# Mask seeds on ScalarE, a split first masked batch, and feed-forward batch 0 begun inside layer one

## The chip, the cores and the metric

The kernel runs on one core of one Trainium2 chip. Its time is the device time of one execution in microseconds (us). Before the change the median of three runs is 509.7 us (509.5 to 510.54). TensorE is called PE here, VectorE DVE, ScalarE ACT, GpSimd POOL, and SP is the queue that issues most of the DMAs.

## The reference

Eight batches of 256 tokens with 128 features go through four residual blocks:

```python
x = x + xattn0(layernorm(x), ctx)          # layer one: 16 heads of 8, no mask
x = x + ffn0(layernorm(x))                 # quantised linear, 3-tap conv, SiLU, quantised linear
x = x + xattn1(layernorm(x), ctx, mask)    # layer two: logits + mask * -1e9
x = x + moe(layernorm(x))                  # 8 experts, top 2 of them per token
```

`ffn0` rounds the layer-normed activations to integers per token (`act_quant`), multiplies by ternary weights into 512 hidden channels, convolves each channel over three neighbouring tokens, applies SiLU, rounds again and multiplies back to 128. In `xattn1` every logit gets `mask * -1e9` before its softmax.

## The kernel before

Every engine runs one hand-written program in order; semaphores are the only ties between engines. What stands later in an engine's program cannot start before what stands ahead of it, so the order of the lines is the schedule.

**Attention.** `attention_tensor`, `attention_scalar`, `attention_vector`, `attention_gpsimd` and `attention_sync` each run bodies b = -1, 0, ... 7 and a tail (b = 8, 9). A body has 16 steps n, one for a head. The table `STEPS` says at which step each other stage of a body is issued, one number for each layer. In step n PE computes `scores(b+1, n)` (L1658, two matmuls of 128x256 into banks 0 and 1 of PSUM), from which DVE takes the row maxima (L1289; L1303 with a mask in layer two). Once per half batch POOL splits these maxima (L817, L819), PE transposes them (L1635), ACT copies them (L967) and a DMA writes them into the stack of queries. Then `shifted(b, n)` recomputes the scores transposed, with the maxima subtracted (L1743, banks 2 to 4), ACT takes the exponential (L1023), and PE multiplies four heads at once with the values (`weighted_v`, L1698). In layer two `shifted` first puts the mask there: one matmul of 128x512 (L1740) with `start=True`, and the two of L1743 add to it. Between these stand, once per batch, the projections of queries and keys (L1618, L1619; high parts on ACT, L1052, or L954 outside the loop; low parts on DVE, L1313) and of values (L1781), the normalised output's transposes (L1852, L1860) and projection (L1867), which makes the new residual (L1282). Its layer norm is made by DVE (statistics, L428 to L434), POOL (`ln_power`, L439, L441) and DVE again (`ln_apply`, L447); in layer one quantising follows on DVE (L458 to L462) and POOL (L468 to L474).

**Feed-forward.** `ffn_tensor`, `ffn_scalar`, `ffn_vector` and `ffn_rows`/`quant_clip` on POOL run one step for a batch: hidden products (L1671 and, with the taps folded into the weights, L1674 to L1676), the conv's middle tap on ACT (L915, L916), its sides on DVE (L924, L930), SiLU on ACT (L940, L944), transposes (L1954), their largest value on DVE (`quant_scale`, L1510), rounding on ACT (L1155), clipping on POOL (L762), transposes back (L1965), copy (L1162), output (L1974), residual on DVE (L1526) and layer norm. PE runs `int_transposes(b-1)`, `ffn_hidden(b+2)`, `output(b-1)`, `tokens(b-2)`, `act_transposes(b+1)` in a step. The last steps are written out; the query and key products of layer two's first batch stand in them (`qk_products(eng, 1, 0, ...)`), and so do its first scores, in front of the values.

**After that** layer two runs the attention loop, with the routing of the experts inside, and a loop over 39 tiles of the experts ends the kernel.

The ties that matter around the change, in `shifted`, `extras` and `ffn_silu`:

```python
if n >= back or after(b, 0):
    eng.wait_ge(a.p_sb, b * 16 + n - back + 1)      # PE: bank free once its last exponential is done
if l == 1:
    eng.matmul(ps[:, bank, :], neg_mask_eye[:, :], mask_k[b % 3]..., start=True, stop=False)
if l == 0 and isinstance(b, int) and b == NB and n == 2:
    eng.wait_ge(a.p_sb, NB * 16)                     # PE: hidden(0) only after layer one's last exponential
    for half in range(2):
        ffn_hidden(eng, 0, 0, half)
```

## Time and profile before

| what | value |
|---|---|
| median of three runs | 509.7 us (509.5 to 510.54) |
| the profiled execution: device time / span from first to last instruction | 508.18 us / 506.4 us |
| granted TensorE clock, mean over the span | 0.981 |
| busy over the span: PE / PEld / DVE / ACT / POOL | 443.3 / 363.2 / 345.9 / 301.6 / 226.5 us |
| layer one's steady bodies | about 32 to 152 us |
| its last body, tail and the start of the feed-forward | 152 to 189.4 us |
| the rest of the feed-forward and the start of layer two | 189.4 to 247 us |
| layer two | 247 to 406 us, a body every 20.9 us |
| experts' tiles | 406 us to the end |

Starts in the trace's timeline are microseconds from the first instruction. A matmul's duration there includes the time that its result takes to pass through; the distance from one start to the next tells what it holds PE for. "[0.58 <-POOL max_split L819]" behind a row says that its engine stood idle for 0.58 us ahead of it and which event ended that.

### The profile page before, as it was taken

How to read it: one execution, taken by the hardware profiler on the slowest of the kernel's cores; microseconds unless marked ns; L12 is line 12 of the kernel's file. 1: busy time of each engine (PE TensorE's matmuls, PEld its weight loads, DVE VectorE, ACT ScalarE, POOL GpSimd, SP SyncE). 2: the span in 40 equal slices, each digit the busy share in tenths (PEclk: the TensorE clock that was granted, in tenths of full speed). 3: DMA queues.
4: the chain of work that ended last, by engine and by line, in shares of the span. 5: the costliest groups of instructions: out<-in, count | busy, mean ns of one | idle time of the engine just before them, and what ended most of it. 6: DMA issues, size and time to landing. Idle time of an engine off the chain costs nothing.

```text
span 506.4 us, 11481 instructions
## 1 busy us (share of the span) xinstructions
PE 443.3 (88%) x3709; PEld 363.2 (72%) x3709; DVE 345.9 (68%) x1233; ACT 301.6 (60%) x649; POOL 226.5 (45%) x455
## 2 busy tenths in 40 slices
PE   3689999999998779967999999999999889899960
PEld 2477777777775668856778878777777579899960
DVE  6767787878783267877887788787878266444424
ACT  5237776767767448874466756566556555455630
POOL 4752464123216245767200225354453566666650
PEclk9999999999999989989999999999999999999995
DMA  6463323332405995034253234333320301332107
GB/s 216 150 223 105 115 85 116 102 101 77 137 4 207 426 415 213 2 105 130 84 159 113 88 107 158 118 122 94 112 61 2 87 23 39 85 85 82 53 15 249
DMA packets 40698, 61.55 MB, mean 122 GB/s; under 512 B 6121, under 2 KB 30506, under 8 KB 39232
## 3 DMA queue, kind: packets, MB, share of 16 engines
q1 hardware_dynamic: 38080, 56.20, 34.0%
q0 software_dynamic: 2272, 4.24, 2.6%
q8 instruction: 30, 0.49, 0.4%
q10 hardware_dynamic: 288, 0.39, 0.3%
q14 instruction: 28, 0.23, 0.2%
HBM read 31.45 MB, written 29.23 MB: 120 GB/s over the span
## 4 chain that ended last, share of the span: by engine, by line
PE 45%; DVE 10%; issue 5%; ACT 4%; DMA 3%; SPq 2%; POOL 1%; POOLq 0%; DVEq 0%; ACTq 0%
PE ps L1698 6%; PE ps L1658 6%; PE ps L1740 6%; PE ps L1743 5%; PE ps L1889 5%; PE ps L1900 5%; ACT probs L1023 2%; PE ps L1867 1%; DMA k_blocks<-y_dram 1%; DVE ps L1303 1%; PE ps L1954 1%; PE ps L1674 1%; SPq L544 1%; PE ps L1675 1%; PE ps L1676 1%
## 5 line engine op out<-in xcount | busy, mean ns | idle before, releaser
L1023 ACT ACTIVATE probs<-ps 128x512 f32<-128x512 f32 x256 | 147.0, 598 | 79.6 <-PE ps L1743 75.0
L1658 PE MATMUL ps<-k_blocks,q_stacks 128*128 128x256 f32 x512 | 117.9, 314 | 6.4 <-DVE row_max L1289 3.0
L1289 DVE TENSOR_REDUCE row_max<-ps 128x2 f32<-128x512 f32 x144 | 94.9, 686 | 26.9 <-PE ps L1658 25.7
L1743 PE MATMUL ps<-q_stacks,k_blocks 128*128 128x256 f32 x512 | 104.9, 288 | 1.2 <-DMA q_stacks<-maxT 1.0
L1303 DVE CUSTOM_DVE_ANT_0 ps<-ps,mask_q 128x256 f32<-128x256 f32 x224 | 89.8, 452 | 20.6 <-PE ps L1658 18.9
L1743 PEld LDWEIGHTS ps<-q_stacks,k_blocks 128*128 128x128 f32 x512 | 86.8, 189 | 20.8 <-issue 10.6
L1658 PEld LDWEIGHTS ps<-k_blocks,q_stacks 128*128 128x128 f32 x512 | 82.6, 197 | 13.9 <-issue 4.3
L1698 PE MATMUL ps<-probs,v_aug 128*32 128x256 f32 x1024 | 68.5, 385 | 4.3 <-ACT probs L1023 3.1
L817 POOL TENSOR_SCALAR max_split<-row_max 128x16 fp32r<-128x16 f32 x32 | 6.5, 204 | 124.3 <-issue 93.0
L1740 PE MATMUL ps<-mask_k,neg_mask_eye 128*128 128x512 f32 x128 | 54.5, 426 | 0.0
L739 POOL DMA_INDIRECT y_dram<-x_ring x39 | 39.1, 1003 | 22.6 <-ACT x_ring L1102 14.2
L1698 PEld LDWEIGHTS ps<-probs,v_aug 128*32 128x32 f32 x1024 | 27.8, 109 | 24.1 <-ACT probs L1023 6.2
L1889 PE MATMUL ps<-m_xT,m_w 128*128 128x128 f32 x312 | 41.8, 277 | 2.9 <-DVE m_w L1449 1.7
L1900 PE MATMUL ps<-conv_out,m_h 128*128 128x128 f32 x312 | 41.2, 276 | 0.0
L1889 PEld LDWEIGHTS ps<-m_xT,m_w 128*128 128x128 f32 x312 | 37.9, 192 | 4.1 <-DVE m_w L1449 3.0
L1455 DVE COPY conv_out<-experts 128x512 f32 x39 | 18.3, 469 | 31.2 <-PE ps L1900 31.1
L729 POOL DMA_INDIRECT slots_dram<-rows,r_slot x32 | 32.4, 1011 | 13.8 <-issue 7.8
L1900 PEld LDWEIGHTS ps<-conv_out,m_h 128*128 128x128 f32 x312 | 37.9, 192 | 0.0
L1740 PEld LDWEIGHTS ps<-mask_k,neg_mask_eye 128*128 128x128 f32 x128 | 24.0, 188 | 12.8 <-issue 11.9
L1303 DVE DVE_READ_ACCUMULATOR2_ANT row_max<- 128x1 f32 x224 | 31.9, 142 | 0.0
L439 POOL TENSOR_SCALAR ln_ve<-ln_mv 128x2 f32<-128x2 f32 x24 | 5.8, 240 | 52.4 <-DVE ln_mv L434 52.3
L1090 ACT ACTIVATE m_xT<-ps 128x128 f32<-128x128 f32 x39 | 10.8, 277 | 25.1 <-PE ps L1880 25.1
(217 smaller groups left out, 760.1 us busy)
## 6 DMA issues: line engine op xcount, KB each, us to landing
slots_dram<-x_ring SPq DMA_DIRECT2D x1, 10400.0 KB, 30.1
q_stacks<-q_dram SPq DMA_DIRECT2D x32, 256.0 KB
k_blocks<-k_dram SPq DMA_DIRECT2D x128, 48.0 KB
q_dram<-qk_parts SPq DMA_DIRECT2D x16, 256.0 KB, 2.9
k_dram<-qk_parts SPq DMA_DIRECT2D x16, 256.0 KB, 2.9
mask_in<-host_mask SPq DMA_DIRECT2D x8, 512.0 KB, 3.6
experts<-host_experts SPq DMA_DIRECT2D x1, 4096.0 KB, 39.1
x_ring<-slots_dram SPq DMA_DIRECT2D x39, 65.0 KB
```

The source lines that it names most:

```text
L729: eng.indirect_dma_start(out=slots_dram[:, :], out_offset=bass.IndirectOffsetOnAxis(ap=r_slot[r][:, k, i:i + 1], axis=0), in_=rows[:, r, k ...
L739: eng.indirect_dma_start(out=y_dram[:, :], out_offset=bass.IndirectOffsetOnAxis(ap=x_ring[:, slot, D:D + 1].bitcast(U32), axis=0), in_=x_r ...
L1023: eng.activation(probs[:, n // HPS % 2, n % HPS, :, :].rearrange("p k q -> p (k q)"), ps[:, head_bank(BANKS_T, n)[0], :], ACT.Exp).then_in ...
L1289: eng.tensor_reduce(row_max[:, :, n], ps[:, head_bank(BANKS_S, n)[0], :].rearrange("p (i k) -> p i k", i=NT), AX.X, ALU.max).then_inc(a.s_ ...
L1303: last = eng.tensor_tensor_reduce(out=scored, in0=scored, in1=mask_q[t % 2][:, i, :], scale=1.0, scalar=-3.0e38, op0=ALU.add, op1=ALU.max, ...
L1455: eng.tensor_copy(m_down[:, j % 2, :, :].rearrange("p c d -> p (c d)"), experts[:, bass.ds(weight_at[j] + EH, EC * D)]).then_inc(m_weights, 1)
L1658: mm = eng.matmul(ps[:, bank, i * S:(i + 1) * S], q_stack[r][:, st, i * P:(i + 1) * P], k_blocks[r][:, st, j, :], start=not masked, stop=n ...
L1698: mm = eng.matmul(ps[j * HR:(j + 1) * HR, bank, 0:S], v_aug[r][:, k, first:first + HR], probs[:, st % 2, j, k, :], start=(odd == 0 and k = ...
L1740: eng.matmul(ps[:, bank, :], neg_mask_eye[:, :], mask_k[b % 3][:, :, :].rearrange("p i k -> p (i k)"), start=True, stop=False)
L1743: mm = eng.matmul(ps[:, bank, k * S:(k + 1) * S], k_blocks[r][:, st, j, k * P:(k + 1) * P], q_stack[r][:, st, :], start=(l == 0), stop=(l ...
L1889: mm = eng.matmul(ps[:, BANK_W[j % 2], c * P:(c + 1) * P], m_w[:, j % WR, c * P:(c + 1) * P], m_xT[:, j % 2, :], start=True, stop=True)
L1900: mm = eng.matmul(ps[:, BANK_Y[j % 2], 0:D], m_h[:, j % 2, c, :], m_down[:, j % 2, c, :], start=(c == 0), stop=(c == EC - 1))
```

## The change

Seven edits, in the order in which they run:

1. In layer one the transposes of the second half's maxima move from step 0 to step 1, behind `shifted(b, 1)` and ahead of the last `weighted_v` of the batch before; ACT's copy of that `weighted_v`'s result moves from step 0 to step 1.
2. In layer one `ln_apply` moves from DVE to POOL.
3. `ternary_taps` (three POOL operations) moves from body 6 to body 3.
4. The feed-forward's hidden products of batch 0 move into the last body of layer one (chunks 2 and 3 at step 3, chunk 0 at step 6, chunk 1 at step 8); the conv's middle tap of batch 0 goes to DVE, the load of the SiLU table stands right behind the last exponential, and hidden products of batch 1, transposes and `quant_scale` of batch 0 go into the tail.
5. The keys of layer two's batch 0 are projected in feed-forward step 3 and its queries in step 4 (`first_product` into the free half of bank 7, `first_high`, `first_low`, `first_side`), and the product of both in step 5 is gone.
6. The scores of batch 0's heads 0 to 7 are spread over the last three feed-forward steps, their maxima on DVE with them.
7. In layer two, for heads 5, 7, 8, 11, 13 and 15 of each batch the mask matmul on PE is replaced by an ACTIVATE that writes `-MASK_A * mask_k` into the bank (`mask_seed`), on which the two matmuls add; they wait for it.

```diff
-    "max1": (0, 2),
+    "max1": (None, 2),
-    "a_out1": (0, 0),
+    "a_out1": (1, 0),
-    "d_ln": (11, 12),
+    "d_ln": (None, 12),
+        SEEDED = (5, 7, 8, 11, 13, 15)
+        SEED_STEPS = (2, 4, 5, 8, 10, 12)
+        FIRST_SIDES = {3: 1, 4: 0}
...
         attention_gpsimd, body:
                     ln_power(eng, s, b - 1)
+                    if l == 0:
+                        ln_apply(eng, s, b - 1)
-            attention_gpsimd(eng, 0, "main 0", {-1: add_output_bias, 0: routing_constants, 1: ternary, NB - 2: ternary_taps})
+            attention_gpsimd(eng, 0, "main 0", {-1: add_output_bias, 0: routing_constants, 1: ternary, 3: ternary_taps})
...
         attention_scalar, behind the exponential of step n:
+                    if l == 1 and exists(b) and n in SEED_STEPS:
+                        mask_seed(b, SEEDED[SEED_STEPS.index(n)])
+            def mask_seed(b, n):
+                if n == SEEDED[0]:
+                    eng.wait_ge(a.k_k, b + 1)
+                eng.wait_ge(a.p_sb, b * 16 + n - 2 if n < H - 1 else b * 16 + 12)
+                eng.activation(ps[:, head_bank(BANKS_T, n)[0], :],
+                               mask_k[b % 3][:, :, :].bitcast(F32).rearrange("p i k -> p (i k)"),
+                               ACT.Copy, scale=-MASK_A).then_inc(a.t_seed, 1)
...
         attention_tensor, shifted:
-                if l == 1:
+                seeded = l == 1 and n in SEEDED
+                if seeded:
+                    eng.wait_ge(a.t_seed, b * len(SEEDED) + SEEDED.index(n) + 1)
+                elif l == 1:
                     eng.matmul(ps[:, bank, :], neg_mask_eye[:, :], mask_k[b % 3][:, :, :].rearrange("p i k -> p (i k)"),
                                start=True, stop=False)
         attention_tensor, body and extras:
+                    ahead = l == 0 and n == at["pv"] % HPS and exists(b)
+                    if ahead:
+                        shifted(b, r, n)
+                        second_max(b)
+                if l == 0 and b == NB - 1 and n == 3:
                     eng.wait_ge(a.s_max, NB * 16)
+                    eng.wait_ge(f_tern, 9)
+                    ffn_hidden(eng, 0, 0, 1)
+                if l == 0 and b == NB - 1 and n in (6, 8):
+                    ffn_hidden(eng, 0, 0, 0, (n // 2 - 3,))
+                if l == 0 and b == NB and n == 2:
                     eng.wait_ge(a.p_sb, NB * 16)
-                    eng.wait_ge(f_tern, 9)
-                    for half in range(2):
-                        ffn_hidden(eng, 0, 0, half)
-                if l == 0 and isinstance(b, int) and b == NB and n == 8:
-                    ffn_hidden(eng, 1, 1, 0)
+                    ffn_hidden(eng, 1, 1, 1)
+                if l == 0 and b == NB and n == 4:
+                    ffn_hidden(eng, 1, 1, 0, (0,))
...
         ffn_tensor, step:
+                if b in FIRST_SIDES:
+                    eng.wait_ge(fx_new, b - 1)
+                    first_product(eng, FIRST_SIDES[b])
                 if exists(b + 2):
                     ffn_hidden(eng, b + 2, r, 0)
                     ffn_hidden(eng, b + 2, r, 1)
+                if b in FIRST_SIDES:
+                    eng.wait_ge(att[1].qk_lo, 2 - FIRST_SIDES[b])
                 if exists(b - 1):
                     output(b - 1)
...
-            qk_products(eng, 1, 0, BANKS_HEAD[0])
```

**PE, layer one, steps 0 and 1 of a middle body.** `k_blocks,q_stacks` are scores and `q_stacks,k_blocks` shifted scores, `ident_r,max_split` is the transposes of the second half's maxima, and `probs,v_aug` the last `weighted_v` of the batch before. Before:

```order
L1658 MATMUL ps<-k_blocks1,q_stacks 128x256 x2
L1743 MATMUL ps<-q_stacks,k_blocks0 128x256 x2
L1635 MATMUL ps<-ident_r,max_split 8x128 x4
L1658 MATMUL ps<-k_blocks1,q_stacks 128x256 x2
L1698 MATMUL ps<-probs,v_aug1 32x256 x8
L1743 MATMUL ps<-q_stacks,k_blocks0 128x256 x2
```

After:

```order
L1743 MATMUL ps<-k_blocks1,q_stacks 128x256 x2
L1841 MATMUL ps<-q_stacks,k_blocks0 128x256 x2
L1743 MATMUL ps<-k_blocks1,q_stacks 128x256 x2
L1841 MATMUL ps<-q_stacks,k_blocks0 128x256 x2
L1720 MATMUL ps<-ident_r,max_split 8x128 x4
L1783 MATMUL ps<-probs,v_aug1 32x256 x8
L1743 MATMUL ps<-k_blocks1,q_stacks 128x256 x2
L1841 MATMUL ps<-q_stacks,k_blocks0 128x256 x2
```

The transposes and `weighted_v` moved behind the scores and the shifted scores of head 1.

**PE, from the last `weighted_v` of layer one to its projection.** `ffn_w` and `w1_taps` are the feed-forward's hidden products (two matmuls of `ffn_w` or three of `w1_taps` for a chunk or half of one), `ident,o_raw` and `ident,o_norm` transposes of the attention's output, `ident,probs` the transposes of the feed-forward's activations, `w_all,o_normT` the projection. Before:

```order
L1676 MATMUL ps<-xnT_all,w1_taps 128x255
L1671 MATMUL ps<-xnT_all,ffn_w 128x256 x2
L1852 MATMUL ps<-ident,o_raw 128x128 x4
L1860 MATMUL ps<-ident,o_norm 128x128 x2
L1674 MATMUL ps<-xnT_all,w1_taps 128x256
L1675 MATMUL ps<-xnT_all,w1_taps 128x255
L1676 MATMUL ps<-xnT_all,w1_taps 128x255
L1674 MATMUL ps<-xnT_all,w1_taps 128x256
L1675 MATMUL ps<-xnT_all,w1_taps 128x255
L1676 MATMUL ps<-xnT_all,w1_taps 128x255
L1867 MATMUL ps<-w_all,o_normT 128x128 x2
```

After:

```order
L1783 MATMUL ps<-probs,v_aug1 32x256 x8
L1756 MATMUL ps<-xnT_all,ffn_w 128x256 x2
L1955 MATMUL ps<-ident,o_raw 128x128 x4
L1759 MATMUL ps<-xnT_all,w1_taps 128x256
L1760 MATMUL ps<-xnT_all,w1_taps 128x255
L1761 MATMUL ps<-xnT_all,w1_taps 128x255
L1963 MATMUL ps<-ident,o_norm 128x128 x2
L2056 MATMUL ps<-ident,probs 128x128 x8
L1759 MATMUL ps<-xnT_all,w1_taps 128x256
L1760 MATMUL ps<-xnT_all,w1_taps 128x255
L1761 MATMUL ps<-xnT_all,w1_taps 128x255
L1970 MATMUL ps<-w_all,o_normT 128x128 x2
```

Batch 0's hidden products, whose last two rows stand first in the fence of before, are gone from here; batch 1's are spread between the transposes, and batch 0's activations are transposed ahead of the projection.

**ACT, layer two, behind the exponential of head 1 of a middle body.** `probs<-ps` is an exponential, `ps<-mask_k` a seed, `maxT<-ps` the copy of the second half's maxima, `qk_parts` the high parts of a later batch, `v_aug` its values. Before:

```order
L967 ACTIVATE maxT<-ps 8x512
L1023 ACTIVATE probs<-ps 128x512 x2
L1052 ACTIVATE qk_parts<-ps,b_all 128x512 x2
L1023 ACTIVATE probs<-ps 128x512 x4
L1036 ACTIVATE o_normT<-ps 128x256
L1043 ACTIVATE v_aug0<-ps 128x2x16x8
L1023 ACTIVATE probs<-ps 128x512 x2
```

After:

```order
L1016 ACTIVATE maxT<-ps 8x512
L1072 ACTIVATE probs<-ps 128x512
L1131 ACTIVATE ps<-mask_k1 128x512
L1072 ACTIVATE probs<-ps 128x512
L1103 ACTIVATE qk_parts<-ps,b_all 128x512 x2
L1072 ACTIVATE probs<-ps 128x512
L1131 ACTIVATE ps<-mask_k1 128x512
L1072 ACTIVATE probs<-ps 128x512
L1131 ACTIVATE ps<-mask_k1 128x512
L1072 ACTIVATE probs<-ps 128x512 x2
L1087 ACTIVATE o_normT<-ps 128x256
L1094 ACTIVATE v_aug1<-ps 128x2x16x8
```

Three seeds came in, behind the exponentials of heads 2, 4 and 5; three more stand in the second half of the body, behind those of heads 8, 10 and 12.

## Rows read from the trace of the kernel before

**Rows 1.** Busy by stretch (stretch, length, five engines, PEclk, DMA share, GB/s)

```profile
32.00:152.00 120.00, 112.70 (x1063) 87.86 (x1063) 95.66 (x220) 84.81 (x169) 38.94 (x82) 1.00 0.32 97
...
189.40:247.00 57.60, 47.96 (x337) 40.65 (x335) 43.67 (x132) 38.20 (x82) 36.49 (x59) 0.96 0.30 101
...
285.40:306.30 20.90, 20.79 (x184) 16.36 (x178) 17.12 (x88) 12.97 (x28) 4.90 (x19) 1.00 0.37 113
...
388.00:406.00 18.00, 14.44 (x131) 10.32 (x123) 6.61 (x41) 9.92 (x23) 10.43 (x31) 1.00 0.24 61
```

**Rows 2.** Waits of PE, 32 to 152 us (in total, times, longest)

```profile
PE ps L1635 <- POOL max_split L819: 3.1, 6, 0.6
```

**Rows 3.** Timeline, layer one, steps 0 to 1 (start, us, engine, line)

```profile
101.67 0.40 PE L1743 MATMUL ps<-q_stacks,k_blocks 128*128 128x256 f32 x2
...
102.65 0.41 PE L1635 MATMUL ps<-ident_r,max_split 128*8 128x128 f32 x4 [0.58 <-POOL max_split L819]
...
103.38 0.69 DVE L1289 TENSOR_REDUCE row_max<-ps 128x2 f32<-128x512 f32 x1 [0.81 <-PE ps L1658]
```

**Rows 4.** Groups by line and shape (count, busy, mean ns, idle before)

```profile
L1023 ACT ACTIVATE probs<-ps 128x512 f32<-128x512 f32 x256 | 147.0, 598 | 79.6 <-PE ps L1743 75.0
...
L1740 PE MATMUL ps<-mask_k,neg_mask_eye 128*128 128x512 f32 x128 | 54.5, 426 | 0.0
...
L447 POOL TENSOR_SCALAR xn<-x_res,ln_mv,ln_rstd 128x128 f32<-128x128 f32 x16 | 12.7, 798 | 0.9
...
L1155 ACT ACTIVATE probs<-ps,fa 128x512 f32<-128x512 f32 x16 | 10.2, 703 | 3.0 <-DVE fa L1520 3.0
...
L447 DVE TENSOR_SCALAR xn<-x_res,ln_mv,ln_rstd 128x128 f32<-128x128 f32 x16 | 4.8, 344 | 3.1 <-POOL ln_rstd L441 2.5
```

**Rows 5.** Timeline, POOL and DVE side by side, end of the feed-forward

```profile
238.24 1.58 POOL L447 TENSOR_SCALAR xn<-x_res,ln_mv,ln_rstd 128x128 f32<-128x128 f32 x2
...
238.32 1.29 DVE L1289 TENSOR_REDUCE row_max<-ps 128x2 f32<-128x512 f32 x2 [0.23 <-PE ps L1658]
```

**Rows 6.** Waits of PE, 152 to 190 us

```profile
PE ps L1698 <- ACT probs L1023: 2.7, 3, 1.2
```

**Rows 7.** Timeline, tail of layer one and start of the feed-forward

```profile
168.40 1.07 PE L1698 MATMUL ps<-probs,v_aug 128*32 128x256 f32 x16 [1.20 <-ACT probs L1023]
...
172.95 0.60 PE L1852 MATMUL ps<-ident,o_raw 128*128 128x128 f32 x4
...
177.27 0.61 PE L1867 MATMUL ps<-w_all,o_normT 128*128 128x128 f32 x4
...
180.63 0.60 DVE L447 TENSOR_SCALAR xn<-x_res,ln_mv,ln_rstd 128x128 f32<-128x128 f32 x2 [1.27 <-POOL ln_rstd L441]
```

**Rows 8.** Timeline, feed-forward step 5

```profile
216.86 0.59 PE L1618 MATMUL ps<-xnT_all,w_all 128*128 128x256 f32 x2
...
217.73 0.61 PE L1974 MATMUL ps<-w,f_intT 128*128 128x128 bf16 x8
217.93 1.27 ACT L954 ACTIVATE qk_parts<-ps,b_all 128x512 fp32r<-128x512 f32 x2 [0.51 <-PE ps L1619]
```

**Rows 9.** Timeline, a body of layer two

```profile
303.12 0.40 PE L1740 MATMUL ps<-mask_k,neg_mask_eye 128*128 128x512 f32 x1
...
303.36 0.40 PE L1743 MATMUL ps<-q_stacks,k_blocks 128*128 128x256 f32 x2
...
314.71 0.14 DVE L1303 DVE_READ_ACCUMULATOR2_ANT row_max<- 128x1 f32 x1
...
314.90 0.50 PE L1658 MATMUL ps<-k_blocks,q_stacks 128*128 128x256 f32 x2
```

**Rows 10.** Timeline, the last body of layer two

```profile
396.80 0.71 PE L1867 MATMUL ps<-w_all,o_normT 128*128 128x128 f32 x4 [0.33 <-ACT o_normT L1036]
...
399.98 1.58 ACT L1023 ACTIVATE probs<-ps 128x512 f32<-128x512 f32 x3
...
405.01 0.60 DVE L1359 TENSOR_SCALAR rows<-x_res,ln_mv,ln_rstd 128x128 f32<-128x128 f32 x2 [6.00 <-POOL ln_rstd L441]
```

More of the change, by code:

```diff
@@ L496, in stack_landed, with first_side @@
             eng.wait_ge(stack_loaded[half][part], (a.first + b + 1) * STACK_COUNT[part] * DMA)
+        def first_side(eng, a, w):
+            dst = (q_dram[0][:, DH:HR, :], k_dram[0])[w].rearrange("h (d w) q -> h d w q", w=3)
+            eng.wait_ge(a.qk_hi, 2 - w)
+            eng.dma_start(dst[:, :, w:w + 2, :], qk_parts[:, 4 * w:4 * w + 2, :].bitcast(F32)).then_inc(a.to_dram, DMA)
+            eng.wait_ge(a.qk_lo, 2 - w)
+            low = 2 - 2 * w
+            eng.dma_start(dst[:, :, low:low + 1, :], qk_parts[:, 2 + w:3 + w, :].bitcast(F32)).then_inc(a.to_dram, DMA)
+            hold(eng, a.to_dram, (2 - w) * 2 * DMA)
+            for half in range(2):
+                sets = slice(2 * half, 2 * half + 2)
+                if w == 0:
+                    q_load(eng, 0, half, sets)
+                else:
+                    k_loads(eng, 0, half, sets)
         def parts_store(eng, a, t):
@@ L1615, in pre_transposes, with first_product @@
             mm.then_inc(ln_pre.xT, 1)
+        def first_product(eng, w):
+            if w == 1:
+                eng.wait_ge(att[0].mT_sb, NB * 2)
+                eng.wait_ge(wq_scaled, 2)
+            else:
+                eng.wait_ge(ln_f0.xs, 1)
+                eng.wait_ge(att[1].qk_lo, 1)
+            eng.matmul(ps[:, BANK_M, S:2 * S], (wq, wk)[w][1][:, :], one((xnT_all, ctxT)[w], 0),
+                       start=True, stop=True).then_inc(att[1].qk_ps, 1)
         def qk_products(eng, l, t, bank):
@@ L1667, in ffn_hidden @@
             x = one(xnT_all, b)
-            for c in range(2 * half, 2 * half + 2):
+            for c in chunks or range(2 * half, 2 * half + 2):
                 h = hidden_ps(r, c)
```

177 lines of the change are left out of this document (105 added, 72 removed).

## The prediction

> **What bounds the kernel now.** I read the busy time by stretch first [rows 1]. In a steady body of layer two PE is busy for 20.79 of 20.90 us at full clock (1.00), DVE for 17.12, ACT for 12.97: PE sets the length and ACT has 7.9 us to spare. In layer one's steady bodies PE is busy for 112.70 of 120 us, so a few waits remain. In the feed-forward (189.4 to 247 us) no engine passes 48 of 57.6 us: chains through all engines decide there. In the last body of layer two (388 to 406 us) there are no scores any more, PE is busy for 14.44 of 18 us and waits for ACT and for POOL.
>
> Then the waits. Layer one's largest wait of PE is the one for POOL's split of the maxima, 3.1 us in six waits [rows 2]; the timeline of one body shows it as the 0.58 us ahead of the transposes, while DVE stands idle 0.81 us until the scores behind them [rows 3]. The groups by line give prices [rows 4], the timelines show the places. Idle time of ACT in layer two is no reserve lying in one piece: 75.0 of its 79.6 us ahead of exponentials are waits for PE's shifted scores [rows 4], a slice of each head.
>
> **Layer one's transposes (edit 1).** PE now has the scores and shifted scores of head 1 ahead of the transposes. From 101.67 the old row order gave 0.40 us of work and then 0.58 us of wait; the new order puts two pairs there, some 0.7 us, and the split is done by then. The scores come 1 us earlier than before, so DVE's 0.81 us gap closes too. What comes late next is the copy of the maxima on ACT, wanted only by the second half of the body. I take 0.5 us for each of six bodies (of 0.58): **-3.0 us**. Bounds: 0, if the maxima that the next body waits for end no earlier, and 6 x 0.81 = -4.9, if DVE was the chain.
>
> **ln_apply on POOL (edit 2).** Per batch two operations of 344 ns leave DVE and two of 798 ns come to POOL [rows 4]: the result is 0.9 us later. In the steady bodies nobody waits: DVE reached its own later than POOL had finished the power, since the operation stood at a step of the body. In the tail DVE waits for POOL already (its start at 180.63 us) [rows 7], so there +0.95. POOL's queue behind it holds the split of the maxima, several us later.
> The Trainium skill ("SBUF — State Buffer", "SBUF: two separate sides") says that DVE and GpSimd share a port pair that one of them holds for a whole instruction, which speaks against more POOL work; it limits this to DVE operations of certain kinds. Where POOL's 1.58 us of ln_apply and two row maxima ran side by side, these took 1.29 us together [rows 5], no more than one alone twice (0.69 us) [rows 3]. So the trace shows no such stop for the maxima, DVE's main work in layer one. By the rule read without its limit the six bodies and the last one would lose up to 7 x 1.6 = 11 us; that is a rival below, with a small chance.
>
> **Ternary taps (edit 3).** Some 5 us of POOL move to a body where POOL is mostly idle (38.94 of 120 us) [rows 1]: 0.
>
> **Start of the feed-forward (edit 4).** Between the last weighted_v (168.40) and the projection (177.27) lie 8.9 us [rows 7]: 1.0 of weighted_v, 3.55 of hidden(0) up to the transposes at 172.95 (eight pieces of 0.44: three for each of two chunks, one for each of the other two), then these, a wait for the normalising, its transposes, and six pieces of hidden(1). In the new order this stretch holds 1.0 + 0.9 (two pieces) + 0.45 (four transposes) + 1.3 (three pieces, filling the wait) + 0.3 + 1.0 (the activations' eight transposes) + 1.3 (three pieces) = 6.2 us: -2.7. Hidden(0) is 3.5 us in the body before, which has 2.7 us of waits for exponentials [rows 6]; its chunks at steps 3, 6 and 8 meet only part of them, and ACT, which sets that body's pace there, gets its shifted scores a little later. So at least 0.8 comes back, and I take 1.4. With the +0.95 of ln_apply the chain to the first layer-normed batch gains 0.35; the activations' transposes ahead of it gain more. I take **-0.6 us** at the start of the steps, between -2.5 (transposes decide) and +1.5 (the chain through POOL decides, and a PE that waits more runs at a lower clock: 0.96 in the stretch behind) [rows 1].
>
> **First batch split (edits 5 and 6).** Step 5 loses the products (216.86 to 217.73, 0.87 us on PE) and the high parts on ACT (1.27 us) [rows 8] that stood ahead of the rounding chain, and the low parts on DVE: I take -1.4 of these. Steps 3 and 4 each gain one product of 0.43 us, one ACTIVATE of half the size on ACT and one operation on DVE, and output waits for the latter: +0.5 each. SP's loads for the first half of the heads leave earlier and nobody waits for them. The scores spread over the last steps fill PE's waits, but three more row maxima of 0.69 us stand ahead of the last residual on DVE; the last output waits for its copy anyhow. I take -0.5 for that. Together -1.4 + 1.0 - 0.5 = **-0.9 us**, between -2 and +1.5 (the new wait for the low parts holds PE's queue, with output, tokens and transposes behind it, in both steps). The chain from the last residual through POOL to the first shifted scores is unchanged and moves as a whole.
>
> **Seeds (edit 7).** A mask matmul holds PE from 303.12 to 303.36 [rows 9], 0.24 us; six a body are 1.44, and 48 in all are 11.5. What they cost ACT no row shows: no ACTIVATE here writes PSUM. From below it is the distance of exponentials back to back, 1.58 us for three [rows 10], 0.49 each; from above the rounding's 703 ns of the same size [rows 4]. I take 0.55, near the exponentials, the same 128x512 in the other direction. That is 3.3 us a body, 12.97 + 3.3 = 16.3 of some 19.9 us: ACT stays under PE. Each seed stands three steps ahead of its head but cannot run before that bank's exponential; PE reaches the head two heads later, over 2 us, so its wait on the seed is normally over. Behind a seed on ACT wait the next exponential and, behind that, weighted_v.
> Yet not all is gained. The scores of head 7 start at 314.90, right behind DVE's row maximum of 314.71 [rows 9]: in that part DVE decides, and what head 5 saves is lost. Of heads 7 and 8 I count 0.35, of heads 11, 13 and 15 0.6, as exponentials pushed back by a seed delay weighted_v there. 0.95 for each of seven bodies is -6.65. In the last body PE waits for exponentials and gains nothing from less work; seeds of heads 13 and 15 (2 x 0.5, and 0.25 for their own waits) stand ahead of the rank copy, from which POOL's chain runs to the rows at 405.01, for which DVE stood idle 6.00 us [rows 10]: +1.25. Sum **-5.4 us**, between -11.5 and +4 (each seed holding PE for 0.08 us more than it saves).
> The Trainium skill ("ScalarE: Activation LUTs", "Step-by-step: what each stage is for") says that ScalarE reaches PSUM faster than SBUF. No row of this case shows it; by it the seeds would sit at the lower bound of 0.49 us or under it, ACT would have 0.4 us a body more to spare, and the sum would move towards the first rival's.
>
> **Sum.** -3.0 - 0.6 - 0.9 - 5.4 = -9.9 us. The profiled execution took 508.18 us (506.4 span and 1.8 around it); it becomes 498.3. The median of the runs stands 1.5 above it, so 509.7 - 9.9 = **499.8 us**. The experts' tiles, with no edit, only move.
>
> **Rivals.**
> 1. The seeds are paid in full: PE is busy without a gap in layer two [rows 1], so each removed matmul shortens the body. Seven bodies save 7 x 1.44 = 10.1, the last one loses 0.5: -9.6 in place of -5.4, 495.6 us. Against it: row maxima that PE already waits for [rows 9].
> 2. ACT and DVE take the seeds' gain back, layer two 0: total -4.5, 505.2 us. For it: DVE is at 17.12 of 20.9 and not evenly spread; against it: 7.9 us of idle ACT.
> 3. The edges lose: body 7 and the POOL chain give +1.5, steps 3 and 4 +1.5, in place of -1.5 together; 504.3 us.
> 4. Slower than before: the seeds make ACT's order the bound. Shifted scores wait in PE's queue for the seed, behind them the scores for DVE, and the exponential that frees the bank stands behind the seed again. It decides from the point where each seed holds PE for 0.24 + 4.5/48 = 0.33 us; at a whole seed, 0.55, it is 48 x 0.31 = +15, less 4.5: 520 us; at 0.45 it is 515.
> 5. POOL's ln_apply stops DVE, as weighed above: 11 - 9.9 = +1, 511 us.
>
> **Chances.** My forecast (497 to 503) 0.52, rival 1 0.15, rival 2 0.14, rival 3 0.09, rival 4 0.07, rival 5 0.03. About 1 us (0.2%) is what can be told from no change here. Slower: rivals 4 and 5 but for some of 5, 0.08; within 0.2%: the rest of 5 and the poor end of rivals 2 and 3, 0.04; faster 0.88. The range runs from below rival 1 to above rival 2, 494 to 506.5: outside lie rivals 4 and 5 and the full sum of all lower bounds.
>
> **What would show it.** Right: layer two's bodies at about 19.9 us with PE still busy nearly throughout, ACT at 16 us, seeds of about 0.55 us; no wait for the split in layer one and bodies 0.5 us shorter; the last body of layer two longer by a microsecond, with POOL's slots later. Wrong: shifted scores that wait for ACT's seeds, scores that wait for row maxima more than before, bodies still at 20.9 us, a DVE that stands while POOL applies the norm, or steps 3 and 4 longer by more than 1 us.

## The result and the profile after

The changed kernel takes 506.12 us (median of 5 runs, 504.78 to 507.69), the kernel before 510.54 us (5 runs, 509.5 to 511.55): ratio 0.9924, 95% interval 0.9899 to 0.9949. By the ratio that is some 3.9 us less, by the two medians 4.4. Forecast were 9.9 us less and 499.8 us. The profiled execution of the changed kernel took 505.85 us with a span of 504.0 us, 2.4 us less than the span of before.

The busy time by stretch, with the columns of [rows 1], in stretches that answer to those:

```profile
32.00:152.00 120.00, 115.06 (x1076) 89.55 (x1075) 94.69 (x211) 87.06 (x173) 53.92 (x100) 1.00 0.32 97
...
190.00:245.00 55.00, 46.10 (x329) 39.08 (x329) 41.95 (x128) 34.56 (x73) 35.61 (x58) 0.96 0.28 92
...
282.60:302.90 20.30, 19.87 (x180) 15.25 (x174) 17.01 (x88) 15.98 (x34) 4.90 (x19) 1.00 0.37 111
...
384.00:403.00 19.00, 12.96 (x117) 8.90 (x120) 5.83 (x38) 13.70 (x30) 10.00 (x27) 0.98 0.24 62
```

A steady body of layer two takes 20.4 us now, not 20.9 and not the 19.9 that I had forecast. ACT is at 15.98 us in it (16.3 forecast), and PE, which was busy for all but 0.1 us, stands idle for 0.43. In the stretch of the last body, taken 1 us longer here, PE is busy for 1.5 us less and ACT for 3.8 us more.

I took the starts of a few marks from the timelines of two executions of each kernel (the second of each is an experiment below) and set the distances from one mark to the next side by side. "Projection" is the matmuls of L1867, which stand at L1970 after the change; "activations" the transposes of L1954, L2056 after. All in us:

| from, to | before, 1st | before, 2nd | changed, 1st | changed, 2nd |
|---|---|---|---|---|
| start to layer one's first projection | 59.08 | 61.24 | 59.13 | 58.17 |
| five bodies of layer one | 86.50 | 86.47 | 84.15 | 84.12 |
| two more projections (last body, tail) | 31.69 | 31.70 | 31.04 | 31.03 |
| last projection to activations of batch 2 | 16.65 | 15.60 | 18.22 | 18.46 |
| to the last residual of the feed-forward | 41.38 | 40.99 | 39.79 | 39.78 |
| to layer two's first projection | 39.70 | 39.70 | 40.18 | 40.18 |
| five bodies of layer two (the fifth is shorter) | 103.40 | 103.29 | 100.68 | 100.72 |
| to the next-to-last projection | 18.40 | 18.37 | 18.38 | 18.37 |
| to the last projection | 15.13 | 17.28 | 18.53 | 18.50 |
| to the end | 94.47 | 94.46 | 93.90 | 94.37 |
| span | 506.4 | 509.1 | 504.0 | 503.7 |

Most rows repeat within about 0.1 us. Three do not for one and the same kernel: the start (up to 2.2 us), the stretch behind layer one's last projection (1.05 us), and the one to the last projection (2.15 us); two more, the one to the last residual and the one to the end, differ by 0.4 to 0.5 us in one of the kernels.

The lines behind the rows that changed, in the order of the program. Steps 0 and 1 in a body of layer one, as in [rows 3] (timeline: start, duration, engine, line):

```profile
100.87 0.48 PE L1743 MATMUL ps<-k_blocks,q_stacks 128*128 128x256 f32 x2
...
101.20 0.23 POOL L855 TENSOR_TENSOR max_split<-row_max,max_split 128x16 fp32r<-128x16 f32 x1
...
101.57 0.39 PE L1720 MATMUL ps<-ident_r,max_split 128*8 128x128 f32 x4
```

POOL's split ends at 101.43, while PE still works on head 1, and the transposes follow without a wait. The waits of [rows 2] are gone; the largest that is left of PE's waits between 32 and 152 us is for row maxima (total, times, longest), and it was there before the change with 2.1 us:

```profile
PE ps L1743 <- DVE row_max L1349: 1.9, 6, 0.4
```

The start of the feed-forward, against [rows 7]:

```profile
168.23 1.07 PE L1783 MATMUL ps<-probs,v_aug 128*32 128x256 f32 x16 [1.19 <-ACT probs L1072]
...
174.32 0.61 PE L1970 MATMUL ps<-w_all,o_normT 128*128 128x128 f32 x4
...
177.75 1.59 POOL L452 TENSOR_SCALAR xn<-x_res,ln_mv,ln_rstd 128x128 f32<-128x128 f32 x2
...
181.94 1.43 POOL L479 TENSOR_SCALAR xn<-xn,qa 128x128 f32<-128x128 f32 x2 [0.21 <-POOL xn L476]
183.46 0.62 POOL L810 TENSOR_SCALAR mask_k<-mask_in 128x512 fp32r<-128x512 int32 x1
...
183.52 0.44 PE L485 MATMUL ps<-ident,xn 128*128 128x128 f32 x2 [3.26 <-POOL xn L479]
...
184.86 1.31 POOL L796 TENSOR_SCALAR f_int<-probs 128x512 bf16<-128x512 int16 x2
...
185.53 0.61 PE L2068 MATMUL ps<-ident_bf,f_int 128*128 128x128 bf16 x4 [1.57 <-POOL f_int L796]
```

The projection follows the last weighted_v by 6.1 us instead of 8.9. But behind it PE runs out of work: it stands 3.26 us until POOL has applied the norm and quantised batch 7, and 1.57 us more until POOL, after two mask operations, has clipped batch 0's integers. The transposes of these integers follow the projection by 11.22 us; before the change it was 11.32 us in the first trace and 10.59 in the second, with PE at work for most of that time. From there to the activations of batch 2 PE has the same rows of work, but at a lower granted clock (PEclk, the column behind POOL). Before and after:

```profile
188.59:193.92 5.33, 5.33 (x33) 4.70 (x32) 2.72 (x8) 5.01 (x12) 1.23 (x2) 0.82 1.05 450
```

```profile
185.53:192.54 7.01, 6.92 (x32) 5.59 (x33) 1.36 (x4) 3.59 (x8) 1.84 (x3) 0.64 0.99 427
```

In the second traces it is 5.01 us at 1.00 before and 7.27 us at 0.61 after.

The costs of edits 2 and 7, by line and shape (count, busy, mean ns, idle before), against [rows 4]:

```profile
L1838 PE MATMUL ps<-mask_k,neg_mask_eye 128*128 128x512 f32 x80 | 33.7, 422 | 0.0
...
L1131 ACT ACTIVATE ps<-mask_k 128x512 f32<-128x512 f32 x48 | 28.7, 598 | 1.8
...
L452 POOL TENSOR_SCALAR xn<-x_res,ln_mv,ln_rstd 128x128 f32<-128x128 f32 x32 | 25.6, 805 | 1.8
```

A seed takes 598 ns (0.55 forecast) and ln_apply on POOL 805 ns.

A body of layer two, behind the seeded head 11:

```profile
316.70 0.40 PE L1841 MATMUL ps<-q_stacks,k_blocks 128*128 128x256 f32 x2
...
316.93 0.40 PE L1720 MATMUL ps<-ident_r,max_split 128*8 128x128 f32 x4
...
317.32 0.14 DVE L1363 DVE_READ_ACCUMULATOR2_ANT row_max<- 128x1 f32 x1
...
317.51 0.51 PE L1743 MATMUL ps<-k_blocks,q_stacks 128*128 128x256 f32 x2 [0.18 <-DVE row_max L1363]
```

The shifted scores of head 11 start 0.24 us earlier than before within the body, for want of the mask matmul. The next scores then wait 0.18 us, until DVE's row maximum of 317.32 has ended (317.46): the gain is given back on the spot. In [rows 9] DVE was late only at head 7.

The last body, against [rows 10]:

```profile
390.39 0.47 PE L1841 MATMUL ps<-q_stacks,k_blocks 128*128 128x256 f32 x2 [0.48 <-ACT ps L1131]
...
391.57 0.71 PE L1970 MATMUL ps<-w_all,o_normT 128*128 128x128 f32 x4 [0.71 <-ACT o_normT L1087]
...
395.39 0.60 ACT L1131 ACTIVATE ps<-mask_k 128x512 f32<-128x512 f32 x1
...
396.56 1.07 PE L1783 MATMUL ps<-probs,v_aug 128*32 128x256 f32 x16 [1.17 <-ACT probs L1072]
396.88 0.60 ACT L1131 ACTIVATE ps<-mask_k 128x512 f32<-128x512 f32 x1
...
397.50 0.19 ACT L1058 ACTIVATE r_rank<-ps 128x24 f32<-128x24 f32 x1
...
400.97 0.60 DVE L1428 TENSOR_SCALAR rows<-x_res,ln_mv,ln_rstd 128x128 f32<-128x128 f32 x2 [7.19 <-POOL ln_rstd L446]
...
401.71 0.41 PE L1947 MATMUL ps<-ident,rows 128*128 128x128 f32 x2 [2.94 <-DVE rows L1428]
```

Here shifted scores wait 0.48 us for a seed, the projection 0.71 us for o_normT, weighted_v 1.17 us for exponentials: ACT is the bound of this body. The rank copy, the rows and their transposes come late through it, as forecast, and PE stands 2.94 us ahead of the transposes (1.95 before).

### The profile page after: what moved, and what is told of

Same layout as the page of the kernel before. It is cut to its first block, busy times and chain, and to the rows that moved or that the text cites. A ratio compares the mean times of both kernels' runs of the same rounds, so it can differ in the third digit from the quotient of the medians.

```text
span 504.0 us, 11484 instructions
## 1 busy us (share of the span) xinstructions
PE 438.4 (87%) x3661; PEld 356.8 (71%) x3661; DVE 340.6 (68%) x1219; ACT 325.5 (65%) x696; POOL 240.6 (48%) x471
## 3 DMA queue, kind: packets, MB, share of 16 engines
q1 hardware_dynamic: 38080, 56.20, 34.3%
## 4 chain that ended last, share of the span: by engine, by line
PE 39%; DVE 14%; issue 6%; ACT 6%; POOL 3%; DMA 2%; DVEq 0%; POOLq 0%; SPq 0%; ACTq 0%
PE ps L1992 6%; PE ps L2003 6%; PE ps L1783 5%; PE ps L1743 5%; PE ps L1841 4%; DVE ps L1363 3%; ACT probs L1072 3%; PE ps L1838 2%; PE ps L1970 1%; DMA k_blocks<-y_dram 1%; DVE ln_st L433 1%; POOL xn L452 1%; PE ps L1759 1%; PE ps L1760 1%; PE ps L1761 1%
## 5 line engine op out<-in xcount | busy, mean ns | idle before, releaser
L1841 PE MATMUL ps<-q_stacks,k_blocks 128*128 128x256 f32 x512 | 106.1, 291 | 1.7 <-DVE row_max L1349 0.8
L1841 PEld LDWEIGHTS ps<-q_stacks,k_blocks 128*128 128x128 f32 x512 | 83.4, 189 | 23.4 <-issue 9.8
L1992 PE MATMUL ps<-m_xT,m_w 128*128 128x128 f32 x312 | 43.3, 283 | 2.1 <-DVE m_w L1518 1.5
L1992 PEld LDWEIGHTS ps<-m_xT,m_w 128*128 128x128 f32 x312 | 39.5, 199 | 2.9 <-DVE m_w L1518 2.1
L1838 PE MATMUL ps<-mask_k,neg_mask_eye 128*128 128x512 f32 x80 | 33.7, 422 | 0.0
L1131 ACT ACTIVATE ps<-mask_k 128x512 f32<-128x512 f32 x48 | 28.7, 598 | 1.8
```

Of the source, the lines that this page charges most:

```text
L1131: eng.activation(ps[:, head_bank(BANKS_T, n)[0], :], mask_k[b % 3][:, :, :].bitcast(F32).rearrange("p i k -> p (i k)"), ACT.Copy, scale=-M ...
L1841: mm = eng.matmul(ps[:, bank, k * S:(k + 1) * S], k_blocks[r][:, st, j, k * P:(k + 1) * P], q_stack[r][:, st, :], start=(l == 0), stop=(l ...
L1992: mm = eng.matmul(ps[:, BANK_W[j % 2], c * P:(c + 1) * P], m_w[:, j % WR, c * P:(c + 1) * P], m_xT[:, j % 2, :], start=True, stop=True)
```

## The experiments

**1. No seeds.** Theory A: the seeds' gain in the steady bodies is half given back to DVE, and in the last body they lose time and bring the half clock at the start of the tiles.

```diff
-        SEEDED = (5, 7, 8, 11, 13, 15)
-        SEED_STEPS = (2, 4, 5, 8, 10, 12)
+        SEEDED = ()
+        SEED_STEPS = ()
```

> The changed kernel without seeds (all 128 mask matmuls on PE again); every other edit stays. Theory A (DVE's row maxima give back half of what the seeds save in the steady bodies, and in the last body the seeds lose 1.2 us and bring a second stretch of half clock at the start of the experts' tiles): steady bodies of layer two go back from 20.36 to about 20.9 us (+3.7 in seven bodies), the last body is 1.2 us shorter, the half clock at 402 to 409 us is gone (-2.2): the whole within 1 us of the changed kernel, 505 to 507 us. Rival B (the seeds are worth what PE saves, and something else in the change lost the time): 6 us or more above the changed kernel, 511 us or more. Rival C (the half clock at 402 us comes from the work of the earlier stages, not from the seeds): it stays, and the time is 508 to 509 us.

Measured: 509.24 us (7 runs, 507.5 to 510.25), ratio to the kernel before 0.9961 (0.9937 to 0.9984); theory A had 505 to 507, rival C 508 to 509. Five bodies of layer two take 103.31 us as before the change, so the seeds are worth 2.63 us in five bodies, 0.53 each. From the fifth of these bodies' projection to the last one it is 35.48 us without and 36.91 with seeds: they cost 1.43 us there. But the half clock stays without them. The granted clock between the last two projections, in this run and in the changed kernel (PEclk is the column behind POOL):

```profile
396.20:413.60 17.40, 14.53 (x107) 11.27 (x107) 5.89 (x26) 8.18 (x23) 9.09 (x28) 0.80 0.26 66
```

```profile
391.60:410.10 18.50, 14.03 (x103) 10.53 (x103) 5.89 (x26) 10.05 (x24) 8.30 (x24) 0.82 0.24 61
```

So the half clock comes without seeds, too: the last part of theory A is wrong and rival C right on it. That the seeds have no share in it is not shown by this run (runs 7 and 8).

**2. The last batch without seeds.**

```diff
-                    if l == 1 and exists(b) and n in SEED_STEPS:
+                    if l == 1 and 0 <= b < NB - 1 and n in SEED_STEPS:
-                seeded = l == 1 and n in SEEDED
+                seeded = l == 1 and n in SEEDED and b < NB - 1
```

> The changed kernel with seeds in batches 0 to 6 only; the last batch has its mask matmuls on PE. Theory A: steady bodies stay at 20.36 us, the last body's rows come 1.2 us earlier, the half clock at the start of the experts' tiles goes, 2.2 us more: 3.4 us under the changed kernel, about 502.7 us. Rival C (half clock not from the seeds): 1.2 us under it, 504.9 us. Rival D (in the last body PE waits for exponentials in any case, so nothing changes): 506 us.

Measured: 504.15 us (4 runs, 502.58 to 505.46), ratio 0.9857 (0.9825 to 0.9890), some 2 us under the changed kernel. The steady bodies stay (100.79 us for five), and the last two distances take 17.87 + 16.48 = 34.35 us instead of 36.91. PE's wait for the rows is 1.95 us, as in the kernel before, and not 2.94. The time lies nearer to rival C (504.9) than to A (502.7). Of the 2.56 us between 36.91 and 34.35, 1.43 are the seeds' by run 1; the other 1.13 go with the clock of the last stretch, which was 0.90 here and 0.80 in run 1.

**3 and 4. Less work on DVE, with and without seeds.** The low parts are renewed in 16 of 256 columns and the statistics read 16 of 128, as the expectation says.

```diff
+            e = 16 if l == 1 and t > 1 else S
-                last = eng.scalar_tensor_tensor(out=qk_parts[:, 2 + w, :], in0=ps[:, bank, w * S:(w + 1) * S],
+                last = eng.scalar_tensor_tensor(out=qk_parts[:, 2 + w, 0:e], in0=ps[:, bank, w * S:w * S + e],
-                last = eng.bn_stats(ln_st[:, i, :], x_tile(b, i))
+                last = eng.bn_stats(ln_st[:, i, :], x_tile(b, i)[:, 0:16 if s is ln_a1 else D])
```

> The changed kernel with less work on DVE in layer two: the low parts of queries and keys are renewed in 16 of 256 columns only (for batches 2 to 7) and the statistics of the residual read 16 of 128 columns; so the output is not the reference's. Some 0.9 us of DVE less in a body, in front of the row maxima that scores wait for. Theory A: the gain of head 5's seed, and of head 11's, is no longer given back: steady bodies of some 19.9 us or less, against 20.36. Rival E (ACT's longer queue takes the gain, through o_normT and weighted_v): 20.3 us.

> The kernel without seeds and with the same lighter DVE (same part left out). The control for the run before: theory A wants the seeds to be worth clearly more here than with the full DVE (0.53 us a body), 0.8 to 1.2 us a body between this run and the light one with seeds; this one at about 20.6 us a body. Rival E: the difference stays 0.5 us or falls.

Measured, in a single run each: five bodies take 97.83 us with seeds and 100.44 without (the fifth is a shorter one; a steady body takes 19.7 and 20.2 us). DVE is a bound with or without seeds, since both fell by 0.57 us a body; but the seeds' worth stayed at 0.52. Run 3 alone had the body that theory A forecast; its control, run 4, had what rival E forecast. Taking DVE's side work away does not give the seeds back what they lose; this does not yet tell A from E.

**5 and 6. Lighter row maxima, with and without seeds.** Here the row maxima themselves, not the work between them, are made shorter.

```diff
-                scored = ps[:, head_bank(BANKS_S, n)[0], i * S:(i + 1) * S]
+                scored = ps[:, head_bank(BANKS_S, n)[0], i * S:i * S + S // 2]
-                    out=scored, in0=scored, in1=mask_q[t % 2][:, i, :], scale=1.0, scalar=-3.0e38,
+                    out=scored, in0=scored, in1=mask_q[t % 2][:, i, 0:S // 2], scale=1.0, scalar=20.0,
```

> The changed kernel, but DVE's masked row maxima of layer two (batches 1 to 7) read 128 of 256 columns and start from 20 in place of the lowest number, so the shift in the exponentials is another one. DVE has some 4 us less in a body, evenly over the heads. Theory A (DVE's row maxima, at some 0.77 us a head, are slower than PE without its mask matmul, 0.48 us a head, and give back what the seeds save): bodies of 19.2 to 19.5 us, at least 0.8 under 20.36. Rival E (ACT, or the weight loads that the mask matmul hid on PE): bodies 20.0 us or more.

> The control: the same lighter row maxima without seeds (all masks on PE). Theory A: the seeds are worth 1.0 to 1.4 us a body between this run and the one with them, against 0.53 with the full maxima; this one at 20.5 us, PE's own work. Rival E: they stay worth some 0.5 us.

Measured, in a single run each: 96.52 us for five bodies with seeds, 100.24 without (a steady body takes 19.5 and 20.2 us): the seeds are worth 0.74 us a body, more than 0.53 and less than the 1.0 to 1.4 of theory A. The waits of PE with seeds (262 to 366 us) say what is left; without seeds there is none above 0.15 us:

```profile
PE ps L1970 <- ACT o_normT L1087: 1.4, 5, 0.3
PE ps L1783 <- ACT probs L1072: 0.9, 5, 0.2
```

No wait for row maxima is left; instead PE waits for ACT, 0.28 us a body for o_normT and 0.18 for exponentials. So both theories have their share: DVE takes the gain first, and where DVE doesn't, ACT's longer queue takes some of it. The steps of one body show one more loss: the mask matmul of head 5, first behind weighted_v, held PE for 0.34 us, and now the shifted scores stand there and hold it for 0.34 us and not 0.24, so that the 0.34 us saved there are 0.24.

**7 and 8. Both kernels once more.** No edit.

> The kernel before, unchanged, for a second trace. Theory F (where PE's pauses fall decides from execution to execution whether the clock halves at the start of the experts' tiles, so the 2.2 us that the changed kernel lost there are not the change's): a half-clock stretch may stand near 405 us here too, which the first trace of the kernel before has not, and the projection of the last batch then follows that of batch 6 by 17.3 us in place of 15.1. Rival G (the kernel before never has it): 15.1 us again. The start, to the first projection at 59 us, may differ by 2 us between executions by either.

> The changed kernel, unchanged, for a second trace. Theory F: the half-clock stretch at the start of the tiles may be shorter or gone (16.3 us from one projection to the next in place of 18.5), and the one at the feed-forward's start (182 to 189 us) may be shorter too. Rival G: both as in the first trace, 18.5 us.

Measured: 510.86 and 505.59 us; the distances stand in the table above. One more execution of the kernel before, beside these two, took 506.7 us: single executions of it, 506.7 to 512.42 us over this case, overlap with those of the changed kernel (504.78 to 507.69). The stretch between the last two projections in the first trace of the kernel before, and in the second:

```profile
396.80:411.90 15.10, 11.78 (x106) 8.48 (x106) 5.89 (x26) 8.08 (x21) 8.00 (x22) 1.00 0.30 76
```

```profile
397.36:414.64 17.28, 14.59 (x106) 10.73 (x106) 5.89 (x26) 8.33 (x21) 8.12 (x23) 0.80 0.27 67
```

Same kernel, same work: clock 1.00 and 15.1 us in the one execution, 0.80 and 17.3 us in the other. Theory F holds for the kernel before; the changed kernel was at half clock there both times (18.5 us), as rival G had it. Over all sixteen traces, the seven with all six seeds in the last batch took 18.40 to 18.53 us there at a clock of 0.81 to 0.82. The seven with none took 15.12 to 17.33: one at 1.00, three at 0.90 and three at 0.80 to 0.82. PE's pause ahead of the rows' transposes is 2.94 us with the seeds, and 1.95 without, in the traces at 1.00, at 0.90 and at 0.80 alike; with three seeds a pause of 2.19 us stood beside a clock of 0.81 and one of 2.70 beside 0.90 (runs 13 and 14). So at nearly the same clock the seeds cost some 1.2 us in this stretch. Whether they also make the lower clock likelier stays open.

Behind layer one's last projection the kernel before took 16.65 us with a clock of 0.90, and 15.60 at 1.00 in its second trace. The changed kernel took 18.22 at 0.81:

```profile
174.32:192.54 18.22, 12.73 (x65) 10.16 (x64) 7.41 (x24) 9.03 (x21) 8.79 (x15) 0.81 1.01 417
```

and 18.46 at 0.82 in its second. In the eleven traces in which this part of the changed program is unaltered it took 17.39 to 18.80 us.

**9. Edit 1 undone.**

```diff
-    "max1": (None, 2),
+    "max1": (0, 2),
-    "a_out1": (1, 0),
+    "a_out1": (0, 0),
-                    ahead = l == 0 and n == at["pv"] % HPS and exists(b)
+                    ahead = False
```

> The changed kernel with edit 1 undone (transposes of the second half's maxima and ACT's copy back at step 0). If edit 1 alone made layer one's steady bodies 0.47 us shorter (five of them 84.15 us after, 86.50 before), they are 86.5 us again and the split's waits of 0.58 us are back. Rival: ln_apply's move from DVE to POOL made part of it, as DVE's row maxima then start earlier; then the five bodies take 84.6 to 86.0 us.

Measured, in a single run: 86.13 us for five bodies, against 84.15 with edit 1 and 86.50 before the change, and the waits are back:

```profile
PE ps L1720 <- POOL max_split L855: 2.9, 5, 0.6
```

So edit 1 is worth 1.98 us in five bodies, 0.40 each. The other 0.37 us must come from other edits of layer one; of these only ln_apply's move touches these bodies throughout, but it was not tried alone.

**10 and 11. The chain at the feed-forward's start.** Run 10 puts the last batch's ln_apply back on DVE; run 11 clips batch 0's integers, too, ahead of POOL's quantising of batch 7 and its masks.

```diff
-                    if l == 0:
+                    if l == 0 and b < NB:
                         ln_apply(eng, s, b - 1)            # POOL
                     if l == 0 and n == 0 and b == NB + 1:
+                        ln_apply(eng, s, NB - 1)           # DVE
                         quant_factors(eng, s, NB - 1)
+            quant_clip(eng, 0)                             # POOL, run 11 alone
             attention_gpsimd(eng, 0, "tail")
             attention_gpsimd(eng, 1, "head")
             for b in range(NB):
-                quant_clip(eng, b)
+                if b > 0:
+                    quant_clip(eng, b)
```

> The changed kernel with the last batch's ln_apply of layer one on DVE again (the other batches' stay on POOL). Theory H (the chain through POOL holds the feed-forward's first integers, and PE's pause there, 3.3 and 1.6 us, brings the longer half clock): the transposes of the layer-normed batch 7 come 0.95 us earlier after the last projection (8.2 us instead of 9.2), the first integers too, and the pause of PE is 1 us shorter; with the same half clock the steps start 1 us earlier, 17.3 us after the projection instead of 18.2 to 18.5. Rival: DVE, with quant_scale in its queue, makes nothing of it: 18.2 us again.

> The changed kernel with the last batch's ln_apply on DVE and, on POOL, the clipping of the feed-forward's batch 0 ahead of the quantising of layer one's batch 7 (before, behind it and behind two mask operations). Theory H: the first integers' transposes follow the last projection by 8.5 us instead of 11.2, the steps start 2.0 to 2.7 us earlier (15.5 to 16.5 us after the projection), more if less of it falls in half clock; the whole 2 us under the changed kernel, 504 us. Rival: another wait comes in its place (f_intT's copy on ACT, or hidden(2) that waits for SiLU): under 1 us.

Measured: in run 10, a single run, the transposes of the layer-normed batch follow the projection by 8.50 us instead of 9.20, the first integers by 10.51 instead of 11.21. The steps start after 17.39 us, but that lies at the edge of the eleven traces above (17.39 to 18.80), so it shows no gain by itself. In run 11 the integers come after 9.24 us and the steps start after 15.33, below all of the eleven. From the projection to the feed-forward's last residual it is 55.1 us, against 58.0 in the changed kernel's first trace: 2.9 us less. Of these 1.98 are the integers' earlier start; the other 0.9 lie between them and the activations of batch 2, which take 6.1 us at a clock of 0.72 instead of 7.0 at 0.64. The time is 505.05 us (5 runs, 502.59 to 507.2), ratio 0.9917 (0.9882 to 0.9951): by the runs 1 us under the changed kernel, with intervals that overlap widely; the traces alone show the gain.

**12. Both: the last batch without seeds, and the shorter chain.**

> Both together: the last batch of layer two without seeds, and the shorter chain at the feed-forward's start. If the gains add up, 2.0 (last batch, as measured) and 2.0 (chain) under the changed kernel: 502 us, ratio to the kernel before 0.983. Rival (the half-clock stretches move and take one of them back): 504 us.

Measured: 501.14 us (6 runs, 500.18 to 503.71), ratio to the kernel before 0.9831 (0.9797 to 0.9864). By the medians this version is 5.0 us faster than the changed kernel and 9 us faster than the kernel before. In its trace the last two distances together are 34.3 us, as in run 2, and the steps start 15.3 us after the projection, as in run 11, so neither gain is lost through the other. Its integers follow the projection by 9.24 us:

```profile
174.83 0.61 PE L1973 MATMUL ps<-w_all,o_normT 128*128 128x128 f32 x4
...
178.24 1.31 POOL L796 TENSOR_SCALAR f_int<-probs 128x512 bf16<-128x512 int16 x2
178.54 1.08 DVE L452 TENSOR_SCALAR xn<-x_res,ln_mv,ln_rstd 128x128 f32<-128x128 f32 x2
...
183.82 0.41 PE L485 MATMUL ps<-ident,xn 128*128 128x128 f32 x2 [3.05 <-POOL xn L479]
...
184.07 0.61 PE L2071 MATMUL ps<-ident_bf,f_int 128*128 128x128 bf16 x8
```

POOL clips while DVE applies the norm, and the integers' transposes stand right behind the layer-normed batch's.

**13 and 14. Which seeds pay.** Three of the six seeds each.

```diff
-        SEEDED = (5, 7, 8, 11, 13, 15)
-        SEED_STEPS = (2, 4, 5, 8, 10, 12)
+        SEEDED = (7, 8, 13)         # run 14: (5, 11, 15)
+        SEED_STEPS = (4, 5, 10)     # run 14: (2, 8, 12)
```

> The changed kernel with seeds for heads 7, 8 and 13 alone. The steps of one body, set side by side, say that only these three shorten it (0.06 of head 5 left, 0.24 of heads 7 and 8 together, nothing of 11, 0.24 of 13, nothing of 15, out of 0.53). Theory A (a seed pays only where DVE's row maxima are not what the next scores wait for): five bodies still take 100.7 to 101.0 us, as with six seeds. Rival (each seed pays its 0.09 us): 102.0 us.

> The changed kernel with seeds for heads 5, 11 and 15 alone. Theory A: almost as without seeds, five bodies of 102.9 to 103.3 us (103.3 without seeds). Rival (each seed pays its 0.09 us): 102.0 us.

Measured, in a single run each: five bodies take 100.95 us with the seeds of 7, 8 and 13, and 103.03 with those of 5, 11 and 15; 100.68 with all, 103.31 with none. Both are as theory A had them. The first three carry 2.36 of the 2.63 us. The waits of PE between 262 and 380 us with the other three name who takes head 11's:

```profile
PE ps L1743 <- DVE row_max L1363: 1.0, 6, 0.2
```

In the steps of a body each of the three is some 0.24 us ahead until the next point where PE needs something of DVE's (the values behind the low parts for head 5, the scores behind a row maximum for 11 and 15), and within 0.05 us of the run without seeds behind it. For 5 and 15 the pauses are too short for the list of waits; there it is the place at which the lead is lost that names DVE.

## Why the prediction was wrong

The direction was right, the size was not: 3.9 us instead of 9.9. That the time came out near rivals 2 and 3 (505.2 and 504.3) is partly luck, since each of them happened in part only. Term by term, against the first trace of the kernel before where no other is named:

- **Layer one's transposes, -3.0 forecast.** Right: -2.35 us in five bodies, 1.98 of them edit 1's (run 9). The wait went as described.
- **ln_apply on POOL.** Neutral in the steady bodies, as said, or a little better. In the tail I priced it (+0.95); run 10 gives 0.7 us back. Rival 5 did not occur: the row maxima took 685 ns after and 686 before.
- **Start of the feed-forward, -0.6 forecast: the first step that failed.** The sum for the stretch up to the projection was right (-2.8 us; -2.7 forecast), the last body lost 2.1 instead of 1.4, so the two projections came 0.65 us earlier. But I let the shorter PE program count behind the projection as well, and put a lower clock behind PE's longer wait at nothing in the sum; I had named both only as the bad end of the range. POOL's chain holds the first integers: PE, with its work done earlier, waited 3.3 and 1.6 us for it, and the integers, counted from the last of the five projections, came 0.75 us earlier than in the first trace of before and 0.07 earlier in the second traces. Behind them the same work took 7.0 and 7.3 us instead of 5.3 and 5.0, at a clock of 0.64 and 0.61 instead of 0.82 and 1.00. So the steps start 1.6 us later behind the projection than in the first trace of before, and 2.9 later in the second traces. Together +0.9 to +2.2 in place of -0.6: rival 3 in this part. I had the chain's rows [rows 7] but took its gain as a part of a sum; it was a bound, of which I left out the masks and the clipping that stand behind it in POOL's queue. Run 11 shows it: with the chain cut the steps start 2.1 to 3.5 us earlier than in the eleven traces with the chain as changed. The lower clock went with the longer wait in these traces; that the wait causes it is not shown, as no run changed the wait alone.
- **First batch split, -0.9 forecast.** -1.6 and -1.2 us against the two traces of before, but the start of layer two behind it lost 0.5, and 1.0 without the seeds' gain in its first body (run 1). A stretch at half clock moved from the one into the other: the granted clock is 0.96 and then 1.00 before, 1.00 and then 0.96 after. Both together, without seeds, are -0.6 and -0.2.
- **Seeds, -5.4 forecast: the second step that failed, and the larger one.** -2.63 in five bodies, -0.5 in the first, +1.43 in the last two distances: -1.7. The last body was well foreseen (+1.25; some 1.2 at nearly the same clock). The steady body's 0.95 was mis-sized; it measured 0.53. I had charged DVE with one of the six heads, the one where scores already stood right behind a row maximum [rows 9]. A head without its mask matmul makes PE faster than DVE between two weighted_v, so that DVE becomes late at heads 11 and 15 as well; run 14 shows that three seeds (5, 11, 15) pay 0.06 us a body together, run 13 that the others pay 0.47. DVE's idle time of 3.8 us in [rows 1] was the warning: most of it lies in four pauses of 0.5 to 1.4 us, and between these DVE works nearly without a gap. Rival 2 named this and was given 0.14. Rival 4 did not occur: PE waited for a seed once, 0.5 us in the last body.
- **The tiles "only move".** The next-to-last projection came 5.2 us earlier than in the first trace, the last one 1.8. Of the 3.4 us lost between them some 1.2 are the seeds'; 2.2 are a stretch at half clock that the first trace of before does not have and the second does. Run 1 has it without seeds and run 7 without any edit, so the change is not needed for it; whether the seeds make it likelier is open. Why one execution has it and another not, no run here tells.

## What to carry to other kernels

Where one engine is busy for all of a body, the idle time of the next one, averaged over the body, does not say how much can be gained: take an instruction out and look, step by step, for the next place at which the busy engine would wait; a saving ahead of such a place is worth nothing, and three seeds did nearly the work of six. A transfer of work to an engine that is idle on average must stop where that engine sets the end, here in the last body, where PE had waited for ACT already. And work taken off one engine ahead of a chain through others buys only idle time: follow the chain to its last queue entry before counting it.

## What the runs showed of the hardware that was not expected

- The same kernel showed a granted clock of 1.00 or of 0.80 between its last two projections in two executions, 15.1 and 17.3 us; the start up to layer one's first projection took between 58.2 and 61.5 us over the sixteen traces of this case: at most 59.1 in the eight whose clock was 1.00 there, and 59.5 or more in the eight with 0.86 to 0.97. A term of 2 us read from one trace at such a place has this as its uncertainty.
- An ACTIVATE of 128x512 from SBUF into PSUM took 598 ns, the exponential of the same size from PSUM into SBUF 594 ns in the same trace. The Trainium skill ("ScalarE: Activation LUTs", "Step-by-step: what each stage is for") holds PSUM for the faster destination; between these two, which differ in function and source as well, the runs show no gain from it.
- DVE's ln_apply, two operations from SBUF to SBUF, took 0.59 us with POOL idle (run 10) and 1.08 us beside POOL's clipping (run 12). The Trainium skill ("SBUF — State Buffer", "SBUF: two separate sides") names DVE operations of certain kinds that share a port with GpSimd, and this slowdown agrees with it; the row maxima, which read PSUM, showed nothing of it (685 ns in the mean after the change, 686 before).
- The first shifted scores behind a weighted_v held PE for 0.35 us (from 329.94 to the next start at 330.29 us in the changed kernel) when no mask matmul stood between, and for 0.25 us with one (333.79 to 334.04 in run 1).
